# A four-layer graph network on one core: the last layer's sums turned by VectorE and small transfers, a wide last quarter, and an earlier start of two layers

## The reference

```
x = x + relu(inv_deg * (a*adj + (1-a)*I) @ h @ W.T + b)      # layer 0
x = x + sum over 2 heads of elu(LN(softmax(mask(leaky(s_i + t_j))) @ h_k + h) @ ff1.T) / 2   # layer 1
x = x + relu(softmax(mask(leaky(f_i + g_j))) @ (h @ W))      # layer 2
msg = adj.T @ h                                              # layer 3
x = x + msg * (1 / column sums of adj, 0 where infinite)
```

## Time and profile before

| | |
|---|---|
| median of 3 runs | 1204.41 us (1204.31 to 1205.49) |
| the profiled execution | 1204.87 us |
| its span | 1203.1 us |
| PE busy | 1197.0 us, 99% |
| DVE busy | 894.2 us, 74% |
| ACT busy | 300.6 us, 25% |
| granted TensorE clock | full in all 40 slices |

### The profile page before, as it was taken

How to read it: one execution, slowest core, us unless ns; L and a number is a source line. 1 busy time by engine, 2 the same in 40 slices (tenths; PEclk the granted TensorE clock), 3 DMA queues, 4 the chain that set the end, 5 groups by cost and what they waited for, 6 DMA issues and landing times.

```text
span 1203.1 us, 17391 instructions
## 1 busy us (share of the span) xinstructions
PE 1197.0 (99%) x6634; PEld 850.9 (71%) x6634; DVE 894.2 (74%) x1679; ACT 300.6 (25%) x730; POOL 10.5 (1%) x21
## 2 busy tenths in 40 slices
PE   9999999999999999999999999999999999999998
PEld 9999999954444444444554547999999964444498
DVE  5448675798878888878788887798787779696711
ACT  3312122144323232422323234541212121000000
POOL 3000000000000000000000000000000000000000
PEclk9999999999999999999999999999999999999999
DMA  9888888700110102110000000040303078888910
GB/s 320 295 270 291 294 293 303 254 15 10 44 17 36 18 35 35 53 17 18 3 16 0 18 1 19 2 170 24 140 0 141 1 290 299 301 316 295 324 45 19
DMA packets 66247, 151.66 MB, mean 126 GB/s; under 512 B 22416, under 2 KB 30976, under 8 KB 66176
## 3 DMA queue, kind: packets, MB, share of 16 engines
q1 hardware_dynamic: 53280, 145.43, 34.8%
q10 hardware_dynamic: 12400, 4.72, 1.5%
q0 software_dynamic: 496, 0.55, 0.2%
HBM read 144.33 MB, written 4.24 MB: 123 GB/s over the span
## 4 chain that ended last, share of the span: by engine, by line
PE 96%; DVE 3%; ACT 0%; issue 0%; DVEq 0%
PE acc L491 48%; PE acc L475 37%; PE acc L749 4%; DVE ring L1293 2%; PE mix L557 1%; PE mix L544 1%; PE mix L529 1%; PE turn L506 1%; PE turn L757 1%; PE turn L502 0%; PE mix L615 0%; PE turn L732 0%; DVE stats L1110 0%; ACT U L774 0%; PE turn L625 0%
## 5 line engine op out<-in xcount | busy, mean ns | idle before, releaser
L1293 DVE SCALAR_TENSOR_TENSOR ring<-G,score,mask 128x1024 f32<-128x1024 f32 x384 | 479.1, 1279 | 63.3 <-PE acc L491 32.6
L491 PE MATMUL acc<-ring,G 128*128 128x512 f32 x1024 | 447.2, 593 | 1.0 <-DVE ring L1293 0.7
L491 PEld LDWEIGHTS acc<-ring,G 128*128 128x128 f32 x1024 | 190.5, 190 | 234.7 <-issue 210.3
L475 PE MATMUL acc<-G,ring 128*128 128x129 f32 x2336 | 264.6, 275 | 0.4 <-DVE ring L1293 0.3
L475 PEld LDWEIGHTS acc<-G,ring 128*128 128x128 f32 x2336 | 262.6, 192 | 1.9 <-issue 1.1
L475 PE MATMUL acc<-G,mask 128*128 128x129 f32 x1648 | 186.2, 275 | 0.0
L475 PEld LDWEIGHTS acc<-G,mask 128*128 128x128 f32 x1648 | 185.0, 192 | 0.0
L491 PE MATMUL acc<-mask,G 128*128 128x512 f32 x384 | 166.0, 593 | 0.0
L491 PEld LDWEIGHTS acc<-mask,G 128*128 128x128 f32 x384 | 72.4, 190 | 89.9 <-issue 88.7
L1573 DVE TENSOR_TENSOR ring<-ring,mask 128x1024 f32<-128x1024 f32 x90 | 110.1, 1224 | 8.5 <-DVE ring L1573 0.5
L1331 DVE TENSOR_SCALAR mask<-mask 128x1024 uint8<-128x1024 f32 x103 | 68.4, 689 | 37.3 <-DMA mask<-in_adj_t 37.0
(11 more groups left out here) (213 smaller groups left out, 653.8 us busy)
## 6 DMA issues: line engine op xcount, KB each, us to landing
mask<-in_adj SPq DMA_DIRECT2D x128, 512.0 KB, 5.2
mask<-in_adj_t SPq DMA_DIRECT2D x103, 512.0 KB, 4.8
ring<-in_adj_t SPq DMA_DIRECT2D x18, 512.0 KB, 4.8
G<-given_rows SPq DMA_DIRECT2D x10, 512.0 KB, 4.1
G<-in_adj_t SPq DMA_DIRECT2D x4, 512.0 KB, 5.2
inputs<-V ACTq DMA_DIRECT2D x4, 512.0 KB, 2.7
V<-inputs SPq DMA_DIRECT2D x4, 512.0 KB, 3.9
X<-in_x SPq DMA_DIRECT2D x3, 512.0 KB, 8.5
```

The source lines that it names most:

```text
L475: mm = pe.matmul(acc[:, b, (s % 3) * DW:(s % 3) * DW + DW], lhs[:, s * P:(s + 1) * P], g, start=(k == 0 and s % 3 == 0), stop=(k == T - 1) ...
L491: mm = pe.matmul(acc[:, c, :], g, moving[:, c * BANK:(c + 1) * BANK], start=(k == 0), stop=(k == T - 1), skip_group_check=True)
L1293: dve.scalar_tensor_tensor(E[k % EB], late_home[h] if early and k >= EARLY else rows_home[h, q], rank[h][:, k:k + 1], span(mask, (q * T + ...
```

## The change

Five edits stand in one diff.

1. *Turning in the last layer, quarters 0 to 2.* DVE transposes U in 32 x 32 blocks into the ring's fourth place (`small_turns`, `part_turned`), ACT issues 16 small transfers that bring the blocks back to U (`move_blocks(act, Q + q, range(4))`), and DVE's results read U. PE's eight transposes of these quarters go. DVE's hooks move from tiles 10, 11, 12 to 3 (turn), 15 (divisors), 16 and 17 (results); PE's column product moves from tile 9 to tile 3, except for quarter 1.
2. *The last quarter.* Seven column blocks are multiplied in the wide form, 512 and 384 columns a tile; ACT copies them to U; PE turns them in seven transposes behind tile 9 of the eighth block's loop. DVE adds this quarter's tiles as well, so the column product comes (behind tile 5 of that loop) and the reciprocals are made before the sums; the results are made in three parts (4, 3 and 1 blocks), and SP stores them in three transfers. `weigh_one` goes.
3. *The row vector of layer 1.* `early_of` steps on DVE at tiles 21 and 24 instead of 26 and 28, PE's `spread_top` and `spread_rows` behind tiles 23 and 26 instead of 25 and 28, and DVE's other steps in layer 0's last quarter one to four tiles earlier.
4. *A fifth edge slot* in the first quarter of layers 1 and 3: `idle(0, 2)`, a piece of G that no one reads then, is used for every fifth tile. Row vector 2 of each layer has its home there, so SP loads it only after all sums of quarter 0 (`all_summed(1, 0)`, `all_summed(3, 0)`).
5. *Layer 1's first quarter on DVE.* The steps behind tiles 2, 2, 4, 6, 7, 9, 10, 13, 14, 16, 21, 24, 24, 25, 27, 31 stand behind 4, 4, 6, 8, 9, 11, 11, 14, 15, 16, 22, 23, 25, 26, 27, 29.

```diff
@@ slots and their order
-    E = [ring[:, i, :] for i in EDGE]
+    E = [ring[:, i, :] for i in range(EB)]
+    part_turned = ring[:, 3, :]
+    def edges(h, q):
+        first = fixed(q) and q == 0
+        if h == 1 and first:
+            return [E[2], E[3], idle(0, SPARE), E[0], E[1]]
+        if h == 3:
+            return [E[0], E[1], idle(0, SPARE), E[2], E[3]] if first else [E[2], E[3], E[0], E[1]]
+        return E
@@ move_blocks
+    given, taker = (U[:, 0:QC], flat_v) if q < Q else (part_turned, U[:, 0:QC])
@@ SP
+    sp.wait_ge(*all_summed(1, 0))
+    sp.wait_ge(*all_summed(1, 0))
     load_rows(1, 2)
...
     load_rows(3, 1)
+    sp.wait_ge(*all_summed(3, 0))
     load_rows(3, 2)
@@ PE, layer 0's last quarter and the last layer
-    run(0, Q - 1, {25: lambda: spread_top(early_top[1]), 28: lambda: spread_rows(0)})
+    run(0, Q - 1, {23: lambda: spread_top(early_top[1]), 26: lambda: spread_rows(0)})
...
-        run(4, q, at([3, 9], post3(q - 1)))
-    hooks = at([3, 9], post3(Q - 2))
+        run(4, q, at([9 if q == 1 else 3], post3(q - 1)))
+    hooks = at([3], post3(Q - 2))
     for k in range(T):
-        for b in range(NB):
-            for s in range(3 * b, 3 * b + last_width(b)):
-                mm = pe.matmul(acc[:, b, (s % 3) * DW:(s % 3) * DW + DW], stream3[:, k, s * P:(s + 1) * P], G[:, 0, k, :], ...
+        for c in range(2):
+            n = BANK - c * P
+            mm = pe.matmul(acc[:, c, 0:n], G[:, 0, k, 0:P], stream3[:, k, c * BANK:c * BANK + n], ...
-    pe.wait_ge(post_done, 5 * Q - 1)
+    hooks = at([9, 5], post3(Q - 1))
     for k in range(T):
-        mm = pe.matmul(turn[:, 0:DW], stream3[:, k, (S - 1) * P:S * P], G[:, 0, k, :], ...
+        mm = pe.matmul(acc[:, 2, 0:D], stream3[:, k, (S - 1) * P:S * P], G[:, 0, k, 0:D], ...
@@ ACT, store(q)
     wide_take(q + 4 * Q)
+    move_blocks(act, Q + q, range(4))
     act.wait_ge(post_done, q + 4 * Q + 1)
...
+    act.wait_ge(post_done, 5 * Q - 1)
+    for c in range(2):
+        act.wait_ge(acc_summed[c], 5 * Q)
+        act.copy(U2[:, c, 0:n], acc[:, c, 0:n]).then_inc(acc_taken, 1)
@@ DVE, layer 0's last quarter and layer 1's first
-    stage0(Q - 1, {26: early[0], 28: early[1], 30: ..., 31: ...})
+    stage0(Q - 1, {21: early[0], 24: early[1], 30: ..., 31: ...})
@@ DVE, the last layer
+    def small_turns():
+        dve.wait_ge(acc_taken, taken(4, q + 1))
+        dve.transpose(part_turned, flat).then_inc(small_turned, 1)
+    def first_half():
+        st.wait()
+        dve.wait_ge(blocks_moved, 256 * (Q + q + 1))
...
+    def in_parts():
+        dve.wait_ge(sums_turned, 1)
+        for i, some in enumerate(LAST):
+            if i == len(LAST) - 1:
+                dve.wait_ge(last_summed, 1)
+            results(some).then_inc(last_made, 1)
-    for q in range(1, Q - 1):
-        column_sums(q, at([10, 11, 12], post3(q - 1)))
+    for q in range(1, Q):
+        column_sums(q, at([3, 15, 16, 17], post3(q - 1)))
```

More of the change, by code:

```diff
@@ L1085, in store @@
                 wide_take(q + 4 * Q)
+                move_blocks(act, Q + q, range(4))
                 act.wait_ge(post_done, q + 4 * Q + 1)
                 act.dma_start(span(out.rearrange("(t p) d -> p t d", p=P), q * S, S), V[:, :, :]).then_inc(stored, 16)
-            quarters(act, 0, Q - 2, store)
+            for q in range(Q - 1):
+                store(q)
+            act.wait_ge(post_done, 5 * Q - 1)
+            for c in range(2):
+                act.wait_ge(acc_summed[c], 5 * Q)
+                n = BANK - c * P
+                act.copy(U2[:, c, 0:n], acc[:, c, 0:n]).then_inc(acc_taken, 1)
         @block.vector
@@ L1268, in run @@
                 early = fixed(q) and q == 0 and h in fixes
+                slots = edges(h, q)
+                L = len(slots)
                 if early:
@@ L1598, in divisors, with results @@
                     st.mark(dve.tensor_tensor(inv[:, :], inv[:, :], zero[:, :], ALU.mult))
-                def results(first):
+                def results(some):
+                    for s in range(S)[some]:
+                        sums = flat[:, s * P:(s + 1) * P] if q < Q - 1 else acc[:, 2, 0:D] if s == S - 1 else turn[:, s * P:(s + 1) * P]
+                        ins = dve.scalar_tensor_tensor(V[:, s, :], sums, inv[:, s:s + 1], blocks(X, q, 1, s)[:, 0, :],
+                                                       ALU.mult, ALU.add)
+                    return ins
@@ L1601, in results @@
+                def first_half():
                     st.wait()
-                    dve.wait_ge(sums_turned, q + 1)
+                    dve.wait_ge(blocks_moved, 256 * (Q + q + 1))
                     if q > 0:
                         dve.wait_ge(stored, q * 16)
-                    for s in range(first, first + HALF):
-                        ins = dve.scalar_tensor_tensor(V[:, s, :], turn[:, s * P:(s + 1) * P], inv[:, s:s + 1], blocks(X, q, 1, s)[:, 0, :],
-                                                       ALU.mult, ALU.add)
@@ L1608, in results, with second_half @@
-                    if first:
-                        ins.then_inc(post_done, 1)
-                    else:
-                        st.mark(ins)
-                return [divisors, lambda: results(0), lambda: results(HALF)]
+                    st.mark(results(slice(0, HALF)))
+                def second_half():
+                    results(slice(HALF, S)).then_inc(post_done, 1)
+                def in_parts():
+                    st.wait()
+                    dve.wait_ge(stored, q * 16)
+                    dve.wait_ge(sums_turned, 1)
+                    for i, some in enumerate(LAST):
+                        if i == len(LAST) - 1:
+                            dve.wait_ge(last_summed, 1)
+                        results(some).then_inc(last_made, 1)
```

95 lines of the change are left out of this document (39 added, 56 removed).

## The result

The changed kernel takes **1198.64 us** (median of 5 runs, 1198.28 to 1198.74) where the kernel before, on the same chip, takes 1204.39 us: a ratio of 0.9949, 95% interval 0.9936 to 0.9963. In a second set of five its median was 1198.27. The forecast was 1198.4, in a range of 1196.5 to 1202.6. The profiled execution took 1198.28 us with a span of 1196.5 us, against 1204.87 and 1203.1. VectorE's busy time rose from 894.2 to 936.4 us, PE's fell from 1197.0 to 1191.9. The difference is half a per cent, and the interval leaves out 1.

What follows compares the result with a forecast made beforehand. TensorE was taken as the bound, with 96% of the last chain. Last layer -4.6, layer 1 -1.4 and layer 3 0 make -6.0: 1204.87 to 1198.9, less 0.46 for the median, 1198.4 us; range 1196.5 to 1202.6.

Steps and rivals of the forecast that it cites:

- The last quarter: Last layer on PE: 512- and 384-column instructions replace 129-column ones, 50.4 to 48.3 us, a gain of 2.1.
- the third rival: Last quarter's wide products: a 384-column product costs what 512 does, +6.8 us, 1205.2 in all; chance 0.04.
- PE's turns: Last layer: three groups of eight transposes leave PE (-2.6), seven return (+0.8), one more column product (+0.1); together -1.7 us.
- The tail: After PE's last product: DVE's four small steps go because reciprocals come from the column sums, -0.8 us.
- the last 32 products: End of the last layer on PE: each loses one column, a gain of 0.05 us.
- Is DVE on time: Last layer, fourth column sum on DVE: it ends before PE wants it, with 4.3 us of slack.
- the three signs of being wrong: PE waits for the column product, moves last over 27 us, or layer 1's first quarter is not shorter than 61.5.
- M: Last layer: time the 16 small moves take after DVE's turning; taken as 20 us, between 13.3 and 27.8.
- the price: Last layer: cost of longer moves is 2 x (their time - 25.3) - 4.3 us, nothing below 27.5.
- The rule of packets strictly in turn: Moves beside loads: engines alternate queues packet by packet, so moves take 47 us; doubted, 1237.5 us in all.
- Layer 1's start: Layer 1's first quarter: earlier row vector, shifted DVE steps and fifth slot cut stalls, -1.4 us, bounds 0 and -2.7.
- Layer 3: Layer 3's first quarter: DVE still waits 2.50 us after tile 2, so no gain; 0, bounds -0.3 and +0.3.

Runs made afterwards that it cites:

- the third experiment: The changed kernel, but PE turns the sums with eight transposes again in quarters 0 to 2 of the last layer, without small moves: 1201.14 us.
- the first experiment: The kernel before plus only the early edits (row vector, steps of the first quarters, fifth slot), last layer as before: 1202.79 us, ratio 0.9986.
- the first version of layer 3's steps: The changed kernel with VectorE's first five and late steps in layer 3's first quarter, and PE's second row spread, moved later: 1199.66 us.

## Why the prediction was right, step by step

**The last quarter, 50.4 to 48.3: right.** Measured 48.4. A pair of instructions (512 and 384 columns) takes 2 x 42.17 / 112 = 0.753 us where 0.754 was forecast; the 512 alone are at 0.430 (48.15 / 112), so the 384 columns take 0.323. The line through two rows held, and the third rival (384 costs what 512 does) is out.

**PE's turns, -1.7: right.** -1.6 in the three quarters' pieces and their new neighbours; the third experiment brings 2.5 back for the three that went (2.6 in the sum), and the seven new ones take 0.77 on the chain (0.8).

**The tail, -0.8: right,** 0.78 measured. Last layer together -4.3, against -4.6: the last quarter and the turns give about 0.1 us less each, and the last 32 products did not get the 0.05 that one column was to save but take 0.08 more (64 instructions of 0.113 us, in a loop from 1185.99 to 1194.13).

**Is DVE on time: right.** Its last column sum ends 4.8 us ahead of PE's wish (4.3), its wait ahead of the first results is 3.4 (under 6), and PE waits nowhere in the last layer. None of the three signs of being wrong came: PE doesn't wait for the column product, the moves last 22 us (27 was the limit), and layer 1's first quarter is at 60.4 (61.5).

**M, the moves' time: taken 20, measured 22.0.** It lies between the bounds, and it costs nothing, as the price said for all below 27.5. The 20 was a pick between bounds of 13.3 and 27.8 and not a sum; that the result did not hang on it is the mechanism, shown by 8 more moves. What it took too small is the backlog. Up to 1096 us a move lands 5.6 us (median) after its issue, and the last one, alone in the window from 1095.2 to 1107 us, 10.8 (DMA queues and issues of that window, after):

```profile
q1 hardware_dynamic: 1062, 3.87, 92.0%
q10 hardware_dynamic: 1906, 0.23, 13.3%
...
U<-ring ACTq DMA_DIRECT2D x1, 32.0 KB, 10.8
```

11.75 of issue and 10.8 less the last issue's own 0.7 are the 22. The issue was nearly as forecast (11.3); the landing behind it, taken between 2.0 and 16.5 (27.8 less 11.3), was 10.1.

The rule of packets strictly in turn, which the prediction priced at M = 47 and doubted, fell. In the 11 us of the queue rows above, 2839 packets of moves went beside 806 of loads, 3.5 to one, while the engines were 99% busy; strictly in turn it would be one to one. The Trainium skill ("DMA: Bandwidth & Descriptors", Queues, rings and completion order) has each engine change queues after a whole packet, but its packet is about 9 to 17 descriptors. The prediction took the profile's packets for it, so 47 does not follow from the page. In the profile a move has 272 packets, 17 for each engine, and a load of 512 KB about 144, 9 for each. Counted in whole transfers, 10.4 moves went beside 5.6 loads up to 1096 us, and 7.0 beside 7.4 in the window behind. An estimate from the earlier trace rows (9 x 162 ns + 17 x 11.9 ns for a turn of one load's share and one move's share, 1.7 us) gives M = 27 for 16 moves and 53 for 32, where 22.0 and 35.5 were measured, so strict turns of that unit do not fit either. By what unit the engines do change queues, no run here shows.

**Layer 1's start, -1.4: right in kind, 0.45 small.** Measured -1.85, inside its bounds (0 to -2.7). Up to PE's transposes it was 1.35 (282.00 - 249.67 against 280.20 - 249.22) for a forecast of 1.0; from 295.51 on 0.55 for 0.4. PE enters this quarter 0.45 us earlier in the changed kernel's profile than before, so DVE's times are better read in the first experiment, whose profile enters where the kernel before does. TensorE's timeline there:

```profile
249.65 3.60 PE L504 MATMUL acc<-ring,G 128*128 128x512 f32 x8
...
280.62 1.09 PE L531 MATMUL turn<-ident,G 128*128 128x128 f32 x8
```

In it the first edge tile starts at 245.06 instead of 245.61, 0.55 earlier where 0.9 was forecast (244.42 in the changed kernel's own profile, forecast 244.7). The wait of 0.91 is gone, as forecast. The one new wait has 0.40 us, where 0.9 was charged for new short waits (another, of 0.22, stood there before too). So ACT's second normalisation starts 1.1 us earlier, at 277.39 instead of 278.51, where 0.9 was taken: two terms were off, and their errors nearly cancel. With it ready at 280.57, PE comes to its transposes at 280.62, as soon as its own products let it (280.6 in the prediction); nothing more was to be had there. The experiments add what the prediction did not say: it is slot and steps together. The prediction had given 0.9 of head start to the row vector; it is worth 0.5 by the run without it, and by the first edge tile.

**Layer 3, 0: right for the change as it stands, but the reason was not looked at far enough.** The prediction said that DVE still waits 2.50 us with three tiles made, so "the fifth slot has nothing to fill". So it is; VectorE's timeline, after:

```profile
735.97 0.20 DVE L1441 RECIPROCAL inv<-mix 128x6 f32<-128x6 f32 x1 [2.50 <-PE mix L557]
```

But it was the place of the step, behind tile 2, that kept DVE from getting ahead by the fifth slot. With the first five steps one or two tiles later DVE makes five tiles, comes to that step when PE's product is there (its wait of 2.50 us is gone), and the quarter gets 0.73 us shorter.

**The total is closer than its terms.** -6.0 was forecast and -5.75 measured by the medians; by the traces it is -4.3 and -1.85. The last layer gave 0.3 less and layer 1 0.45 more, and that these cancel is luck.

## What to carry to other kernels

A buffer more and a later schedule are one edit: here the buffer alone measured nothing, the schedule (with the early row vector) 0.15 us, and buffer and schedule together 1.3, even without the row vector. Before moving follow-up steps, look up for each by which tile its result is wanted; those with slack can go, those ahead of a stop cannot. And when work is handed from the critical engine to a chain of others, work out the moment from which their lateness decides: here a transfer of 22 us and one of 28 were hidden, and one of 35 cost 20.

## What the runs showed of the hardware

- *Small moves beside loads.* 16, 24 and 32 moves of 32 KB in packets of 128 bytes took 22.1, 27.7 and 35.5 us (means of two sets) from the turn to the landed columns: 5.6 and then 7.8 for eight more. With 32, the issue itself slowed down, to 1.40 us a move for the first sixteen (22.37 / 16), where it was 0.73 (11.75 / 16) in the changed kernel and 0.66 (10.53 / 16) without loads. That was one set; in the other of that run the two sixteens took 0.79 and 1.01 us a move, and with 24 moves the last sixteen took 0.87 and 0.91. ScalarE's DMA queue with 16 more moves:

```profile
1093.29 22.37 ACTq L1107 DMA_DIRECT2D G<-ring  x16
1115.70 11.96 ACTq L276 DMA_DIRECT2D U<-ring  x16
...
1158.29 10.53 ACTq L1107 DMA_DIRECT2D G<-ring  x16
```

What holds the issue up there was not tried.

- *A wait of TensorE costs clock after it.* With 16 more moves PE waited from 1143.7 to 1153.4 us. Busy times by stretch in that run (from:to, length, PE, PEld, DVE, ACT, POOL, granted clock, DMA share, GB/s):

```profile
1143.60:1146.00 2.40, 0.12 (x1) 0.00 (x0) 2.19 (x3) 0.00 (x0) 0.00 (x0) 1.00 1.00 393
1146.00:1150.00 4.00, 0.00 (x0) 0.00 (x0) 3.69 (x4) 0.00 (x0) 0.00 (x0) 0.78 1.03 416
1150.00:1153.40 3.40, 0.03 (x1) 0.03 (x1) 3.33 (x4) 0.00 (x0) 0.00 (x0) 0.50 0.96 384
1153.40:1157.00 3.60, 3.60 (x7) 1.96 (x8) 3.39 (x3) 0.00 (x0) 0.00 (x0) 0.50 0.49 197
1157.00:1161.00 4.00, 4.00 (x10) 1.95 (x9) 3.79 (x5) 0.00 (x0) 0.00 (x0) 0.82 0.12 20
1161.00:1165.00 4.00, 4.00 (x12) 2.01 (x11) 3.69 (x4) 0.00 (x0) 0.00 (x0) 1.00 0.31 51
...
1205.00:1208.00 3.00, 2.89 (x13) 2.89 (x14) 1.59 (x10) 0.00 (x0) 0.00 (x0) 0.50 0.00 0
```

The granted clock fell to 0.50 (1.2 GHz) during the wait and was back at 1.00 (2.4 GHz) in the stretch from 1161. The 112 products behind the wait took 44.47 us instead of 42.17, 2.3 more, about a quarter of the wait again. The second wait, of 5.32 us up to 1205.11, had the clock at 0.50 behind it too. A wait of 2.46 us in the first version of layer 3's steps left it at 1.00.
